# A fused attention block on one core: where the output projection stands in a step, and who issues two DMAs

## The reference, cut to what matters

```
q = x @ wq + bq;  k = x @ wk + bk;  v = x @ wv + bv        # split in 8 heads of 16
attn = softmax(q k^T / 4)                                  # within each sequence
out = (attn v) @ wo + bo
n = layernorm(x + out, ln1_g, ln1_b)
ff = relu(n @ w1 + b1) @ w2 + b2
result = layernorm(n + ff, ln2_g, ln2_b)
```

## Time and profile before

| | |
|---|---|
| median of 3 runs | 4271.92 us (4266.54 to 4272.6) |
| the profiled execution's own time | 4273.66 us |
| its span | 4271.9 us |
| PE busy | 4104.8 us (96%) |
| PEld busy | 3538.0 us (83%) |
| DVE busy | 3669.8 us (86%) |
| ACT busy | 3434.5 us (80%) |
| POOL busy | 3723.4 us (87%) |
| mean granted TensorE clock | 0.997 of full speed |

### The profile page before, as it was taken

One profiled execution on the slowest core, in us unless ns is written; L12 is line 12 of the kernel. 1 busy time (PEld: TensorE's weight loads), 2 busy tenths in 40 slices (PEclk: granted clock), 3 DMA queues, 4 the chain that ended last, 5 costly groups with the idle time before them and its releaser, 6 DMA issues.

```text
span 4271.9 us, 150528 instructions
## 1 busy us (share of the span) xinstructions
PE 4104.8 (96%) x49930; PEld 3538.0 (83%) x49930; DVE 3669.8 (86%) x9740; ACT 3434.5 (80%) x5890; POOL 3723.4 (87%) x3864
## 2 busy tenths in 40 slices
PE   5999999999999999999999999999999999999997
PEld 4888888888888888888888888888888888888886
DVE  5888888888888888888888888888888888888885
ACT  4888888888888888888878888888888888888886
POOL 4888888888888888988888888888888888888987
PEclk9999999999999999999999999999999999999999
DMA  7788887888888888888778888887878888888883
GB/s 147 178 177 185 175 185 175 186 179 183 180 180 183 178 182 174 184 176 183 177 178 180 183 176 183 176 185 176 187 177 184 180 179 180 180 180 179 186 178 84
DMA packets 1970442, 755.81 MB, mean 177 GB/s; under 512 B 1181312, under 2 KB 1969536, under 8 KB 1969664
## 3 DMA queue, kind: packets, MB, share of 16 engines
q1 hardware_dynamic: 1662480, 605.71, 66.8%
q10 hardware_dynamic: 307184, 140.40, 12.3%
HBM read 202.51 MB, written 134.22 MB: 79 GB/s over the span
## 4 chain that ended last, share of the span: by engine, by line
PE 42%; issue 20%; ACT 10%; DVE 9%; SPq 5%; ACTq 5%; POOL 5%; DMA 3%; DVEq 1%; POOLq 0%
PE bankB L693 10%; PE bankC L693 9%; PE oT_ps L734 6%; SPq L252 5%; PE s_ps L707 5%; PE sT_ps L721 4%; ACT h_sb L397 4%; DMA stack<-parts 3%; PE bankC L670 3%; DVE xT_sb L502 2%; ACT parts L385 2%; PE bankA L670 2%; ACTq L430 2%; ACT parts L379 2%; PE bankB L670 2%
## 5 line engine op out<-in xcount | busy, mean ns | idle before, releaser
L417 ACT ACTIVATE prob_sb<-sT_ps 128x1024 f32<-128x1024 f32 x1024 | 1050.6, 1026 | 415.8 <-PE sT_ps L721 342.4
L547 DVE TENSOR_REDUCE max_sb<-s_ps 128x8 f32<-128x1024 f32 x1024 | 1220.2, 1192 | 6.9 <-PE s_ps L707 5.9
L278 POOL TENSOR_TENSOR parts<-rest_sb,parts 128x512 bf16<-128x512 f32 x512 | 584.4, 1162 | 243.0 <-ACT parts L385 243.0
L707 PEld LDWEIGHTS s_ps<-stack 96*128 96x128 bf16 x8192 | 463.9, 98 | 296.1 <-issue 181.4
L707 PE MATMUL s_ps<-stack 96*128 96x128 bf16 x8192 | 639.5, 221 | 42.0 <-DMA stack<-parts 24.0
L448 ACT ACTIVATE n_sb<-z_sb,shift,rs 128x128 f32<-128x128 f32 x1024 | 422.2, 483 | 276.1 <-POOL shift L323 276.0
L721 PE MATMUL sT_ps<-stack 99*128 99x128 bf16 x8192 | 627.9, 219 | 2.9 <-ACT prob_sb L417 2.9
L693 PE MATMUL bankB<-w_sb,h_sb 128*128 128x128 f32 x4096 | 525.2, 281 | 77.2 <-ACT h_sb L397 75.8
L693 PEld LDWEIGHTS bankB<-w_sb,h_sb 128*128 128x128 f32 x4096 | 476.5, 191 | 120.5 <-ACT h_sb L397 118.7
L734 PE MATMUL oT_ps<-prob_sb,v_ones 128*32 128x128 f32 x16384 | 554.0, 276 | 4.6 <-ACT prob_sb L417 3.3
L734 PEld LDWEIGHTS oT_ps<-prob_sb,v_ones 128*32 128x32 f32 x16384 | 416.4, 109 | 127.9 <-issue 89.4
(11 more groups left out here) (75 smaller groups left out, 8469.8 us busy)
## 6 DMA issues: line engine op xcount, KB each, us to landing
stack<-parts SPq DMA_DIRECT2D x3072, 128.0 KB, 3.6
x_blocks<-in_x SPq DMA_DIRECT2D x1024, 64.0 KB, 2.4
n_mem<-n_sb SPq DMA_DIRECT2D x256, 256.0 KB, 3.2
n_blocks<-n_mem SPq DMA_DIRECT2D x1024, 64.0 KB, 2.2
out<-out_sb ACTq DMA_DIRECT2D x256, 256.0 KB, 3.3
x_sb<-in_x ACTq DMA_DIRECT2D x255, 256.0 KB, 4.4
stack<-max_parts ACTq DMA_DIRECT2D x768, 8.0 KB, 2.2
h_sb<-in_L_conv_w SPq DMA_DIRECT2D x1, 256.0 KB, 3.1
```

What stands on the lines that cost most here:

```text
L278: pool.tensor_tensor(parts[:, r % 2, 3 * c + LO], rest_sb[:, c], parts[:, r % 2, 3 * c + MID], ALU.subtract).then_inc(lo_split, 1)
L417: act.activation(prob_sb[:, s % 2], sT_ps[:], ACT.Exp, scale=float(D) ** -0.5).then_inc(exp_done, 1)
L547: dve.reduce_max(max_sb[:, (r - lag) % 2, :, s], s_ps[:].rearrange("p (h k) -> p h k", h=H), AX.X).then_inc(max_done, 1)
L707: ins = pe.matmul(s_ps[:, h * P:(h + 1) * P], stack[0:PROD, (r - lag) % 4, 0, h, tok], stack[0:PROD, (r - lag) % 4, 1, h, tok], start=True ...
```

## The change

Three moves; no instruction is added or taken away. On PE, the output projection goes behind `hidden` of chunks 2 and 3. The store of the output goes from the end of ACT's step to SP, one step later (lag 9), between the store of `n_sb` and the loads of x in blocks. On ACT, the load of x goes from behind the copy `xT_parts` to behind the four products of `n_sb`.

```diff
@@ SP
                     sp.wait_ge(n_done, upto(t, r, 5, plus=1))
                     sp.dma_start(n_mem[(r - 5) % 2].rearrange("(s k) m -> k s m", s=SEQS), n_sb[:]).then_inc(n_stored, DMA)
+                if live(t, r, 9):
+                    sp.wait_ge(out_ready, upto(t, r, 9, plus=1))
+                    sp.dma_start(out_g[t + (r - 9)], out_sb[:, (r - 9) % 2]).then_inc(out_stored[(r - 9) % 2], DMA)
                 if live(t, r, -1):
...
-            iterate(sp, step, 0, LEAD, LAST, 5)
+            iterate(sp, step, 0, LEAD, LAST, 9)
@@ ACT
                     act.activation(xT_parts[:, HI], xT_sb[:], ACT.Copy).then_inc(xT_hi, 1)
-                if live(t, r, 0) and (r > 0 or not isinstance(t, int)):
-                    if (v := upto(t, r, 1)) is not None:
-                        act.wait_ge(xb_done, v)
-                    act.dma_start(x_sb[:, r % 2], x_g[t + r]).then_inc(x_loaded[r % 2], DMA)
                 if live(t, r, 7):
                     relu(t, r, 7, 2)
...
                     ins.then_inc(n_done, 1)
+                if live(t, r, 0) and (r > 0 or not isinstance(t, int)):
+                    if (v := upto(t, r, 1)) is not None:
+                        act.wait_ge(xb_done, v)
+                    act.dma_start(x_sb[:, r % 2], x_g[t + r]).then_inc(x_loaded[r % 2], DMA)
                 if live(t, r, 8):
                     apply2(t, r, 8)
...
-                if live(t, r, 8):
-                    act.wait_ge(out_ready, upto(t, r, 8, plus=1))
-                    act.dma_start(out_g[t + (r - 8)], out_sb[:, (r - 8) % 2]).then_inc(out_stored[(r - 8) % 2], DMA)
@@ PE
                 scores_turned(t, r, 0)
+                if live(t, r, 7):
+                    hidden(t, r, 7, 2)
+                    hidden(t, r, 7, 3)
                 if live(t, r, 5):
                     pe.wait_ge(onT_made, upto(t, r, 5, plus=1))
                     pe.wait_ge(v_copied, upto(t, r, 0))
...
                     ins.then_inc(wo_done, 1)
-                if live(t, r, 7):
-                    hidden(t, r, 7, 2)
-                    hidden(t, r, 7, 3)
```

## The result

The changed kernel takes 4346.44 us, the median of four runs (4344.62 to 4354.54), against 4269.95 us for the kernel before beside it. The ratio is 1.0184 with a 95% interval of 1.0171 to 1.0197: 76 us slower, where the forecast was 30 us slower and a range up to 4345. The direction was right, and so was the chain from `z_sb` to exponential 2. Where the loop of work closes was not, and so the size was not.

The account below looks back on a forecast made before the run. PE leads at 96% busy, with the x loop pacing quiet steps. The new z loop's 16.35 plus 0.12 for the stack's waits gives 16.47 per step, +30 us over some 248 steps: 4302 us, range 4258 to 4345.

Parts of the forecast that it names:

- the chain: From `z_sb` through POOL's layernorm, `n_sb` and ACT's `m_sb` to exponential 2: 7.65 us, making exponential 2 0.55 late.
- two-step loop: `down` to next scores of slot 1, `z_sb`, exponential 2, DVE's transpose of x, copy, `down`: 32.70 us, 16.35 per step.
- the floor: New period without disturbances, set by the z loop: 16.35 us per step, equal to the old mean.
- the disturbances: ACT's slow store issues, forecast to count no longer, and PE's waits for the stack's DMAs, 0.12 us per step.
- the x loop: Exponential 2, q, DVE's transpose of x, copy `xT_parts`, `relu`, `down`: 16.14 us before, 16.01 forecast after.
- slow issues: ACT's issue of the output's store, up to 1856 ns, delaying exponential 0; forecast to count no longer.
- the z loop: Loop through the late `z_sb`, exponential 2 and `down`, said to close over two steps and bind: 16.35 us per step.
- The third rival: Slower still: SP becomes late and the stack DMAs start late; period 16.77, 4376 us; chance 0.07.
- Faster: Rival: delay of `z_sb` does not reach exponential 2, so the x loop binds at 16.13, 4217 us; chance 0.14.
- No difference: Rival: the stack's waits go as well, leaving only the floor of 16.35, 4272 to 4278 us; chance 0.17.

Follow-up runs that it names:

- e1: Kernel before with only the projection moved behind both `hidden`, both DMAs left in place: 4345.91 us.
- e4: Kernel after with POOL's power replaced by a multiplication, so the layernorm's scale is not computed: 4237.21 us.
- e7: Kernel before with POOL's power replaced by a multiplication, so the layernorm's scale is not computed: 4268.47 us.
- e3: Kernel after with the projection between `hidden` 2 and `hidden` 3: 4262.70 us.
- e10: Kernel of e9 with the projection between `hidden` 2 and `hidden` 3: 4234.08 us.
- e5: Kernel before with only the output's store moved to SP: 4240.18 us.
- e2: Kernel before with only the two DMAs moved (output's store, load of x), the projection staying first: 4252.85 us.
- e9: Kernel of e5 with the load of x moved behind exponential 1: 4225.77 us.
- e6: Kernel before with only the load of x moved behind n's products: 4257.17 us.
- e8: Kernel before with the load of x and the output's store both issued by ACT behind the first of n's products: 4259.83 us.

## Why the prediction came out as it did

**Right: the chain.** From `z_sb` to exponential 2 the prediction had 7.65, a slack of 0.30 and a delay of 0.85. It is 7.70 after, the delay against PE's scores of slot 1 is 0.94 (from 0.74 ahead of them to 0.20 behind), and exponential 2 follows `m_sb` without a gap. e1 puts the loss in that edit, e4 with e7 in that chain, e3 in the projection's end.

**Wrong: where the loop closes.** The prediction said that the way from `down` to the next scores of slot 1 is "PE alone, 23.88 - 9.06 = 14.82", and so that a late exponential 2 comes back to `z_sb` only after two steps, at 16.35 per step. It is not PE alone, and it takes 14.97 after (2023.61 - 2008.64). The scores of slot 0 reuse `s_ps` and wait for DVE's row maximum of slot 3, which stands behind the rest of q. In the kernel before these two rows stood open to be read:

```profile
2019.05 1.20 DVE L547 TENSOR_REDUCE max_sb<-s_ps 128x8 f32<-128x1024 f32 x1
```
```profile
2020.63 0.45 PEld L707 LDWEIGHTS s_ps<-stack 96*128 96x128 bf16 x8 [0.20 <-issue]
```

The maximum ends at 2020.25 and the scores start at 2020.63: after the 0.06 that the signal takes, 0.32 of slack, less than the 0.55 by which exponential 2 was forecast late. With the rows of before the one-step loop is 7.65 + 1.63 + 2.47 + 1.20 + 0.06 + 3.25 + 0.11 = 16.37. Alone that is no more than 0.02 above the two-step loop. But every error of size now counts in each step and not in every second one, and there were two, both too small: `z_sb` starts 0.20 behind the next scores' matrix multiply and not 0.11, and `z_sb` to `minus_m` takes 2.19 and not 2.14, nearly all of it because `z_sb` itself lasts 0.69 instead of 0.65. Minus 0.03 on the way to the rest of q this gives the 16.48. Neither error is enough by itself: the loop of one step with the forecast's sizes (16.37) adds some 5 us to the forecast, the loop of two steps with the measured sizes (16.42) some 18, and both together (16.48) 33.

**The 46 us that were missing**, worked out: 0.13 per step on the floor (16.48 for 16.35) over 255 steps, 33 us; seven steps more than the 248 that were counted, 1 us; the end of the run, 115.1 us from the last transpose of x (4344.4 - 4229.3) instead of 107.7 (4271.9 - 4164.2), 7 us, which the sum did not have; and some 4 us because the profiled execution lay 3.7 above the median before and at the median after. The two-step loop stands only a hair's breadth below, at (32.70 + 0.14) / 2 = 16.42 by these rows. Where the projection ends one `hidden` earlier, in e3 and e10, a step of 16.10 or 16.11 is the most frequent one; half of the 0.70 that was gained there, added again, gives 16.45.

**Right in size only: the disturbances.** They were put at 0.12 above the floor, all of it for the stack's waits; measured are 16.61 - 16.48 = 0.13. The stack's waits are 17.8 / 223 = 0.08 of it. Another 0.03 is the turn of the hardware loop, which the prediction did not name: two steps there take 20.94 and 18.00 us, 6 us more than two quiet ones. e1 has 0.14 with a quarter of the stack's waits (4.6 us), so the agreement is in part luck.

**The store.** Moved alone, where the x loop binds, it was worth 27 us (e5), slow issues and stack's waits together. Where the z loop binds, both moved DMAs together gave nothing (e1 against after): the exponentials' idle time of this kind fell from 71.3 to 1.4 us, and the waits for the stack rose from 4.6 to 17.8; whether one made up for the other is not shown. SP's pause before the stack was forecast at 0.44 and is 85.4 / 223 = 0.38. The third rival, a time lost at SP, did not show: the kernel after takes no longer than e1, where SP keeps its order.

**The load of x.** That its issue would cost nothing behind n's products was right: it starts 0.15 behind the first of them, and `m_sb` follows 1.55 behind `n_sb` as before. The gain of 0.13 for the x loop is there too. What the prediction gave only to a rival is the price of the transfer in this place: e2 is 13 us slower than e5 though its quiet step is shorter. Why the waits for the stack come back is shown only in part. SP's idle time before the stack goes with the place of the load (e2, e9), yet e6 keeps most of it (SP's wait for POOL there is 246.2 us, against 294.6 in the kernel before in the same stretch) and has 17.9 us of waits for the stack. A loop of 16.01 also leaves the stack 0.13 less time than one of 16.14. How much belongs to each stays open.

**The rivals.** "Faster" fell at the point that was named for it, the slack before exponential 2. "No difference" supposed that the waits for the stack would go with the DMAs; they went from 13.1 to 17.8 us, though the stack's DMAs now land in 2.5 us instead of 3.6. With the store moved alone they did go (e5), so half of that rival's ground was real; but its floor of 16.35 was the forecast's and not the 16.48.

```profile
stack<-parts SPq DMA_DIRECT2D x3072, 128.0 KB, 2.5
```

By the Trainium skill, "DMA: Bandwidth & Descriptors", section "Issuing engines are not separate DMA queues", another issuer saves only the issue's time. e8 and e2 agree: they hold the same transfers in the same stretch from different issuers and differ by 7 us. The Trainium skill, "Advanced Engine Details and Errata", section "Engine Queue Depths", gives ScalarE a queue of 8 instructions on trn2. The load's issue 0.15 behind the start of the first product agrees, as far as one early issue can show it.

## What to carry to other kernels

Before work is moved back on the leading engine, follow what it feeds until it comes back to that engine, and at each link read the slack there, also where engines meet through a buffer that is reused: a loop that looks like one engine's own time may hold a link to another engine with only 0.3 us of slack. A loop that closes in one step makes each misjudged tenth count fully. And a DMA whose issue is taken off a critical queue still moves its bytes somewhere: try its place in the step by itself, since here the store gave 27 us, the load 10, both together 17, and the same two with the load earlier 46.

## What the runs showed of the hardware

The same addition `z_sb` lasted about 650 ns where DVE came to it from other work and about 692 ns where it had waited for PE. In the kernel after all 223 of them waited and take 691 to 693 ns. In the kernel before the 7 of this stretch that had idle time ahead of them take 692 in the median, those without 650. The cause was not looked for. After, between 400 and 4100 us, and before, whole span:

```profile
L590 DVE TENSOR_TENSOR z_sb<-bankA,xb_sb x223: 691/692/693, 412.1 to 4098.5; 128x512 f32<-128x512 f32 x112
```
```profile
L590 DVE TENSOR_TENSOR z_sb<-bankA,xb_sb x256: 639/650/693, 78.8 to 4235.3; 128x512 f32<-128x512 f32 x128
```

ACT issues two DMAs of 256 KB in each step of the kernel before. The issue of the load of x takes 374 to 434 ns in all 255 cases; that of the output's store takes 378 to 1856 ns. Why only the one is slow at times was not looked for.
